# The order of the set-up groups, the split of the layer norm between VectorE and GpSimd, and the layout of inputs in a fused cross-attention and mixture-of-experts kernel

## The reference

```python
h = layernorm(x)
q = (h @ Wq).reshape(b, n, 16, 64)
k = (context @ Wk * 64 ** -0.5).reshape(b, 64, 16, 64)
v = (context @ Wv).reshape(b, 64, 16, 64)
attn = softmax(einsum('bihd,bjhd->bhij', q, k))
o = einsum('bhij,bjhd->bihd', attn, v).reshape(b, n, 1024)
x = x + tanh(g_xattn[0]) * (o @ Wo + bo)
h = layernorm(x)
probs = softmax(h.mean(axis=1) @ gate_w)          # one choice for each of the 2 sequences
top_w, top_i = top_k(probs, 2); top_w /= top_w.sum()
y = sum over the two experts e: top_w[e] * (gelu(h @ w1[e] + b1[e]) @ w2[e] + b2[e])
x = x + tanh(g_ffn[0]) * y
```

## Time and profile before

| | |
|---|---|
| median of 3 runs | 323.33 us (322.87 to 323.44) |
| the profiled execution | 322.94 us, its span 320.8 us |
| TensorE busy | 314.4 us, 98% of the span |
| VectorE busy | 233.7 us, 73% |
| ScalarE busy | 164.1 us, 51% |
| GpSimd busy | 78.8 us, 25% |
| TensorE's granted clock | full in all 40 slices |
| moved in the first three of 40 slices (8.0 us each) | 224, 395 and 197 GB/s |

### The profile page before, as it was taken

How to read it: one execution, slowest core, us unless ns; L and a number is a source line. 1 busy time by engine, 2 the same in 40 slices (tenths; PEclk the granted TensorE clock), 3 DMA queues, 4 the chain that set the end, 5 groups by cost and what they waited for, 6 DMA issues and landing times.

```text
span 320.8 us, 5745 instructions
## 1 busy us (share of the span) xinstructions
PE 314.4 (98%) x1881; PEld 272.1 (85%) x1881; DVE 233.7 (73%) x563; ACT 164.1 (51%) x577; POOL 78.8 (25%) x158
## 2 busy tenths in 40 slices
PE   7899999999999999999999999999999999999996
PEld 7887988988999999988788888888887899888896
DVE  1889997978889999999998475466667554442643
ACT  2548555686766668775466254444533442321320
POOL 1325448484455536335600000000000000000000
PEclk9999999999999999999999999999999999999999
DMA  6992000000000017600007250000020000000011
GB/s 224 395 197 4 2 3 0 0 3 3 0 0 3 0 52 246 230 1 0 2 0 263 55 208 1 0 0 0 8 102 24 2 0 2 0 0 0 2 65 65
DMA packets 20765, 17.35 MB, mean 54 GB/s; under 512 B 11068, under 2 KB 16900, under 8 KB 20612
## 3 DMA queue, kind: packets, MB, share of 16 engines
q1 hardware_dynamic: 20464, 16.51, 17.0%
q10 hardware_dynamic: 276, 0.52, 0.5%
HBM read 14.93 MB, written 2.10 MB: 53 GB/s over the span
## 4 chain that ended last, share of the span: by engine, by line
PE 88%; DVE 7%; DMA 2%; issue 1%; ACT 1%; SPq 0%; DVEq 0%
PE ps L1098 26%; PE ps L1100 26%; PE ps L1099 26%; PE ps L1183 4%; DMA xt<-in_x_dram 2%; PE ps L1272 1%; PE ps L1118 1%; DVE mx L850 1%; PE ps L1156 1%; DVE pT_lo L808 1%; PE ps L1214 1%; PE ps L1370 1%; ACT sx L580 1%; DVE stats L729 1%; DVE sm L819 1%
## 5 line engine op out<-in xcount | busy, mean ns | idle before, releaser
L667 ACT ACTIVATE gel<-ps,b1sel 128x512 f32<-128x512 f32 x64 | 43.9, 690 | 95.5 <-PE ps L1100 95.4
L1057 DVE CAST h_hi<-gel 128x512 fp32r<-128x512 f32 x64 | 28.4, 443 | 58.7 <-ACT gel L667 58.5
L580 ACT ACTIVATE sx<-ps,mx 128x64 f32<-128x64 f32 x128 | 38.3, 327 | 27.6 <-DVE mx L850 27.6
L1098 PE MATMUL ps<-yT_hi,w_hi 128*128 128x512 f32 (+1 forms) x128 | 50.5, 395 | 0.0
L1099 PE MATMUL ps<-yT_lo,w_hi 128*128 128x512 f32 (+1 forms) x128 | 50.0, 390 | 0.0
L1100 PE MATMUL ps<-yT_hi,w_lo 128*128 128x512 f32 (+1 forms) x128 | 49.9, 390 | 0.0
L1059 DVE TENSOR_TENSOR h_lo<-gel,h_hi 128x512 fp32r<-128x512 f32 x64 | 44.9, 702 | 2.2
L466 POOL TENSOR_TENSOR sx<-sx,rs 128x512 f32<-128x512 f32 x32 | 33.2, 1058 | 48.0 <-DVE rs L824 47.8
L1098 PE MATMUL ps<-h_hi,w_hi 128*128 128x512 f32 x96 | 38.4, 400 | 0.0
L1100 PE MATMUL ps<-h_hi,w_lo 128*128 128x512 f32 x96 | 37.5, 390 | 0.0
L1099 PE MATMUL ps<-h_lo,w_hi 128*128 128x512 f32 x96 | 37.4, 390 | 0.0
(11 more groups left out here) (145 smaller groups left out, 672.7 us busy)
## 6 DMA issues: line engine op xcount, KB each, us to landing
stage_w<-in_L_ffn_w_dram SPq DMA_DIRECT2D x7, 1024.0 KB, 7.3
out_dram<-xt SPq DMA_DIRECT2D x6, 256.0 KB, 2.5
wqT<-in_L_xattn_Wq_dram SPq DMA_DIRECT2D x2, 512.0 KB, 7.9
wv_sb<-in_L_xattn_Wv_dram SPq DMA_DIRECT2D x2, 512.0 KB, 9.3
wo_sb<-in_L_xattn_Wo_dram SPq DMA_DIRECT2D x1, 1024.0 KB, 13.7
xt<-in_x_dram SPq DMA_DIRECT2D x1, 1024.0 KB, 10.7
stage_w<-in_L_ffn_w_dram SPq DMA_DIRECT2D x2, 512.0 KB, 4.4
wk_sb<-in_L_xattn_Wk_dram ACTq DMA_DIRECT2D x1, 512.0 KB, 4.2
```

Of the source, the lines that this page charges most:

```text
L580: last = nc.scalar.activation(sx[:, par, c0:c0 + M], ps[:, 2 * par + 1, c0 - BANK:c0 - BANK + M], ACT.Exp, bias=mx[:, par, h:h + 1], accum ...
L667: nc.scalar.activation(gel[:, f % 4, :], ps[:, h_bank, :], ACT.Gelu, bias=b1sel[:, b, slot, f:f + 1]).then_inc(gelu_done, 1)
L1057: nc.vector.tensor_copy(h_hi[:, f % 4, :], gel[:, f % 4, :]).then_inc(hhi_ready, 1)
L1098: mm(acc, hi_w, hi_x, start=start, stop=False)
```

## The change

- Order of the set-up: TensorE, ScalarE and VectorE handle A 0 to 3 before kT 1 and A 4 to 7 behind it. The banks of the groups are dealt out anew. `tg_spread` stands ahead of the first A pair.
- Norm: x's parts are now tiles 0 and 1, 2 and 3, 4 to 7, 8 to 15. VectorE does the norm of tiles 0 and 1 in full, before the statistics of tiles 2 and 3, which move behind the `a_lo` of A 3. For tiles 2 and 3 VectorE does part 0 behind `x_low(1)` and GpSimd the refinements (`newton`) in step -1, behind `xn` of tile 1. The norms of tiles 4 to 7 and 8 to 15 stay where they were and have new numbers.
- Transfers: Wq's first half is issued ahead of Wk's second half, Wq's second half ahead of x tiles 2 and 3.
- Layout: x, Wq, Wk and Wv are laid out in memory, before the launch, so that what one transfer reads lies in one piece. The runs per partition keep their length (2 KB for Wk, Wv and x's parts of two tiles, 4 KB for Wq and four tiles).

```diff
+    def x_block(b, t0, t1):
+        first = next(n for n, (part, u0, u1) in enumerate(_X_BLOCKS) if part == b and u0 <= t0 and t1 <= u1)
+        start = sum(P * (u1 - u0) * D for _, u0, u1 in _X_BLOCKS[:first])
+        return x[start:start + P * (t1 - t0) * D].rearrange("(p t d) -> p t d", p=P, d=D)
...
-        setup_groups = [("ctxT", 0), ("kT", 0), ("kT", 1)]
-        groups = setup_groups + A0 + V0 + late_groups
+        groups = [("ctxT", 0), ("kT", 0)] + A0[:4] + [("kT", 1)] + A0[4:] + V0 + late_groups
-        GRP_BANK = dict(zip(groups, [0, 1, 2, 3, 4, 5, 6, 0, 1, 3, 4, 2, 6, 4, 5, 0, 6] + [0, 1] * len(LATE)))
+        GRP_BANK = dict(zip(groups, [0, 1, 0, 2, 3, 4, 1, 5, 6, 1, 2, 3, 6, 4, 5, 0, 6] + [0, 1] * len(LATE)))
...
-        X_PARTS = [(0, TB // 2), (TB // 2, TB), (TB, NT)]
-        X_BY_DVE = X_PARTS[1][0]
+        X_PARTS = [(0, 2), (2, TB // 2), (TB // 2, TB), (TB, NT)]
+        X_BY_DVE = X_PARTS[2][0]
...
             load_x(0, 0, 0, 2)
-            sp.dma_start(wk_sb[:, :, HD // 2:HD], Wk.rearrange("(k p) n -> p k n", p=P)[:, :, HD // 2:HD]).then_inc(ld_wk[1], 16)
+            sp.dma_start(wqT[:, 0:NP // 2, :], Wq[0]).then_inc(ld_wq[0], 16)
+            sp.dma_start(wk_sb[:, :, HD // 2:HD], Wk[1].rearrange("k p n -> p k n")).then_inc(ld_wk[1], 16)
+            sp.dma_start(wqT[:, NP // 2:NP, :], Wq[1]).then_inc(ld_wq[1], 16)
             load_x(1, 0, 2, TB // 2)
...
+                if s == -1:
+                    newton(*X_PARTS[1], rstd1, ve_x, 2)
                 if s == 1:
-                    newton(*X_PARTS[1], rstd1, ve_x, 2)
+                    newton(*X_PARTS[2], rstd1, ve_x, 3)
                     pool.sem_inc(x_rstd, 1)
...
             group("kT", 0)
+            for g in A0[:4]:
+                group(*g)
             group("kT", 1)
-            for g in A0[:7]:
+            for g in A0[4:7]:
                 group(*g)
...
             x_stats(0, range(0, 2))
-            x_stats(1, range(2, TB // 2))
             x_norm(0)
             dve.wait_ge(tg_spread, 1)
             nc.vector.tensor_copy(tg[:, :], ps[:, 7, 0:2]).then_inc(tg_ready, 1)
-            for g in A0[:6]:
+            for g in A0[:4]:
+                group(*g)
+            x_stats(1, range(2, TB // 2))
+            for g in A0[4:6]:
                 group(*g)
             x_low(0)
             for g in A0[6:]:
                 group(*g)
             x_low(1)
+            x_norm(1)
             x_stats(2, range(TB // 2, TB))
...
                     out_bias(0)
-                    x_norm(1)
+                    x_norm(2)
...
             group("kT", 0)
-            group("kT", 1)
             pe.wait_ge(rows_ready, 1)
             pe.wait_ge(tanh_done, 1)
             mm(ps[:, 7, 0:2], ones_row[:, :], tg_row[:, :], start=True, stop=True).then_inc(tg_spread, 1)
-            for i in range(0, 8, 2):
-                score_pair(i)
+            score_pair(0)
+            score_pair(2)
+            group("kT", 1)
+            score_pair(4)
+            score_pair(6)
...
+    if name == "x":
+        b, s, d = a.shape
+        a = a.reshape(b, 128, s // 128, d)
+        a = _np.concatenate([a[i, :, t0:t1, :].reshape(-1) for i, t0, t1 in _X_BLOCKS])
     if name == "L0_xattn_Wq":
-        a = a.T.reshape(-1, 128, a.shape[0]).transpose(1, 0, 2)
+        a = a.T.reshape(2, -1, 128, a.shape[0]).transpose(0, 2, 1, 3)
+    if name in ("L0_xattn_Wk", "L0_xattn_Wv"):
+        a = a.reshape(a.shape[0] // 128, 128, 2, -1).transpose(2, 0, 1, 3)
```

More of the change, by code:

```diff
@@ L17, in gated_cross_attention_moe_kernel @@
     P = 128
-    B, S, D = x.shape
-    M = ctx_tokens.shape[1]
-    HD = Wv.shape[1]
+    B, M, D = ctx_tokens.shape
+    S = out.shape[0] // B
+    HD = 2 * Wv.shape[-1]
     DH = 64
@@ L38, in gated_cross_attention_moe_kernel @@
     assert 2 * DH == P and 2 * M == P and B * M == P and TOP == 2 and NCH == 2 and KD == 2
-    x_rows = x.rearrange("b (p t) d -> p b t d", t=TB)
+    def x_block(b, t0, t1):
+        first = next(n for n, (part, u0, u1) in enumerate(_X_BLOCKS) if part == b and u0 <= t0 and t1 <= u1)
+        assert _X_BLOCKS[first] == (b, t0, t1)
+        start = sum(P * (u1 - u0) * D for _, u0, u1 in _X_BLOCKS[:first])
+        return x[start:start + P * (t1 - t0) * D].rearrange("(p t d) -> p t d", p=P, d=D)
     out_rows = out.rearrange("(b p t) d -> p b t d", b=B, t=TB)
@@ L350, in load_x @@
             def load_x(i, b, t0, t1):
-                sp.dma_start(xt[:, b * TB + t0:b * TB + t1, :], x_rows[:, b, t0:t1, :]).then_inc(ld_x[i], 16)
+                sp.dma_start(xt[:, b * TB + t0:b * TB + t1, :], x_block(b, t0, t1)).then_inc(ld_x[i], 16)
             sp.dma_start(ctx_sb[:, :], ctx_tokens.rearrange("b m d -> (b m) d")).then_inc(ld_ctx, 16)
             load_x(0, 0, 0, 2)
-            sp.dma_start(wk_sb[:, :, HD // 2:HD], Wk.rearrange("(k p) n -> p k n", p=P)[:, :, HD // 2:HD]).then_inc(ld_wk[1], 16)
+            sp.dma_start(wqT[:, 0:NP // 2, :], Wq[0]).then_inc(ld_wq[0], 16)
+            sp.dma_start(wk_sb[:, :, HD // 2:HD], Wk[1].rearrange("k p n -> p k n")).then_inc(ld_wk[1], 16)
+            sp.dma_start(wqT[:, NP // 2:NP, :], Wq[1]).then_inc(ld_wq[1], 16)
             load_x(1, 0, 2, TB // 2)
             for half in range(2):
-                blocks = slice(half * NP // 2, (half + 1) * NP // 2)
-                sp.dma_start(wqT[:, blocks, :], Wq[:, blocks, :]).then_inc(ld_wq[half], 16)
-            for half in range(2):
                 cols = slice(half * HD // 2, (half + 1) * HD // 2)
-                sp.dma_start(wv_sb[:, :, cols], Wv.rearrange("(k p) n -> p k n", p=P)[:, :, cols]).then_inc(ld_wv[half], 16)
+                sp.dma_start(wv_sb[:, :, cols], Wv[half].rearrange("k p n -> p k n")).then_inc(ld_wv[half], 16)
             load_x(2, 0, TB // 2, TB)
@@ L467, in step @@
                                                 ALU.mult).then_inc(mul_done, 1)
+                if s == -1:
+                    newton(*X_PARTS[1], rstd1, ve_x, 2)
                 if s == 1:
-                    newton(*X_PARTS[1], rstd1, ve_x, 2)
+                    newton(*X_PARTS[2], rstd1, ve_x, 3)
                     pool.sem_inc(x_rstd, 1)
                 if s == 4:
-                    newton(*X_PARTS[2], rstd1, ve_x, 3)
+                    newton(*X_PARTS[3], rstd1, ve_x, 4)
             pool.wait_ge(guess_ready, 1)
@@ L489, in _ @@
         def _(act):
-            act.dma_start(wk_sb[:, :, 0:HD // 2], Wk.rearrange("(k p) n -> p k n", p=P)[:, :, 0:HD // 2]).then_inc(ld_wk[0], 16)
+            act.dma_start(wk_sb[:, :, 0:HD // 2], Wk[0].rearrange("k p n -> p k n")).then_inc(ld_wk[0], 16)
             act.dma_start(gg[:, 0:1], g_xattn.rearrange("(o n) -> o n", o=1)).then_inc(ld_g, 16)
@@ L797, in step @@
                 if s == 4:
-                    x_norm(2)
+                    x_norm(3)
                 if s in (6, 10):
```

1 line of the change is left out of this document (added).

## The result

| | before | after |
|---|---|---|
| median, all runs beside each other | 323.07 us (322.87 to 323.44) | 324.91 us (324.02 to 325.34) |
| the profiled execution | 322.94 us, span 320.8 | 324.02 us, span 322.0 |

The changed kernel is slower: 1.0052 times the time before, interval 1.0037 to 1.0067. That is +1.84 us in the medians, where +0.94 was forecast; 324.91 lies within the range of 323.0 to 325.1 and above the forecast of 324.3. The six runs of before have their median at 323.07, not at the 323.33 of the first three, on which the 324.3 rests; so the forecast of the change is short by 0.9 and not by 0.6. The profiled execution is the fastest of the six; it lies only 1.08 us above the profiled one of before. So two things have to be read: what happens inside the profiled execution, and why most others are later.

What follows compares the result with a forecast made beforehand. VectorE was taken to set the pace up to 45.9 us, TensorE behind it. Terms -0.56 + 1.19 - 0.34 - 0.35 = -0.06, plus 1.0 for the collision, gave +0.94 us: median 324.3, range 323.0 to 325.1.

Steps and rivals of the forecast that it cites:

- The early gain: Set-up: first A pair at 8.1 and fourth at 13.60 instead of 14.16, so VectorE is free 0.56 us earlier.
- Rival 3: Set-up: Wk's second half lands after 9.94, delaying kT's second half and the A groups behind; 324.9 with collision; chance 0.12.
- Rival 2: Set-up: Wq's first half there by 7.7, first A pair at 7.8; 323.0 without collision, 323.9 with it; chance 0.10.
- The additional norm: VectorE behind `x_low(1)`: `x_norm(1)` adds 1.19 us, of which idle times of 0.34 and 0.35 take in part.
- GpSimd: GpSimd's former idle gap: `newton` from 19.5 to 23.2, then `xn` of tiles 2 and 3 from 23.3 to 25.9.
- The collision: VectorE's norm of tiles 4 to 7 falls inside GpSimd's 23.3 to 25.9 and waits: +1.0 us, bounds +0.4 and +1.4.
- Rival 1: Norm of tiles 4 to 7: VectorE's small instructions slip between GpSimd's; -0.06 to +0.4, 323.3 to 323.7 us; chance 0.26.
- My account of its stages: Norm of tiles 4 to 7: first stage +0.2, second +0.4, third and fourth +0.4 us, at least one wait in each.
- the +0.8: Norm of tiles 4 to 7: size by the Trainium skill's rule with three tensor_scalars left out, about +0.8 us.
- for which I take nothing: Input transfers: bytes and runs per partition stay, only places in memory draw together; no gain or loss counted.
- the -0.56: Sum's term for the fourth A pair at 13.60 against 14.16, counted as VectorE being free 0.56 us earlier.
- My reading of the first A pair: Set-up: Wq's first half lands at 8.0, pair starts at 8.1, not before 7.8 as kT's first half is evicted at 7.74.

Runs made afterwards that it cites:

- e2: Changed kernel with GpSimd's four instructions on tiles 2 and 3 cut to 8 of 256 columns: 323.81 us, 1.0023 of the kernel before.
- e1: Changed kernel with VectorE's norm of tiles 2 and 3 moved directly behind their statistics, into VectorE's idle gap: 323.30 us, 1.0009 of the kernel before.
- e3: Kernel before with four linked, unused 128x256 GpSimd instructions added beside VectorE's norm of tiles 4 to 7: 323.77 us, 1.0022 of the kernel before.
- e9: e4 with the norm split, tiles 0 and 1 and part 0 of tiles 2 and 3 before the first `a_lo`: 323.77 us, 1.0025 of the kernel before.
- e8: Kernel before with nine linked GpSimd memsets, which only write, beside VectorE's norm of tiles 4 to 7: 323.17 us, 1.0003 of the kernel before.
- e0: The changed kernel run once more, unchanged: 324.64 us, 1.0064 of the kernel before.
- e7: e1 without the three warm-up products (`warm_up(3)`) ahead of kT: 324.57 us, 1.0027 of the kernel before.
- e6: e1 with x, Wq, Wk and Wv in the old row layout: 323.01 us, 0.9998 of the kernel before.
- e4: Kernel before with the new layout of x, Wq, Wk and Wv alone, old order of work and transfers: 322.13 us, 0.9970 of the kernel before.
- e5: Changed kernel with x, Wq, Wk and Wv in the old row layout: 324.25 us, 1.0043 of the kernel before.
- e10: e1 with the first `warm_up(6)` lengthened to `warm_up(7)`: 323.32 us, 1.0008 of the kernel before.

## Why the prediction was right, point by point, and where a size was off

**The early gain.** The forecast of the steps in the profiled execution holds within 0.16: the first `a_lo` at 9.80 (9.96 forecast), the first A pair at 8.01 (8.1), kT's second half at 10.00 (9.94), the third pair at 12.74 (12.68), the transpose of tile 0 0.54 earlier (0.56). Rival 3, kT's second half too late by its transfer, is out: it waited for nothing. Rival 2, an A pair at 7.8, is out as well: kT's first half was evicted only at 7.92 (7.32 + 0.60).

**The additional norm.** 18.23 to 19.42 is 1.19 us, as forecast, and both idle times of VectorE that were to take it in are filled (the maximum at 20.74, forecast 20.8, without idle before it). e2 against e1 gives 0.5 for it by time.

**GpSimd.** `newton` from 19.42 to 23.06 (19.5 to 23.2), `xn` of tiles 2 and 3 from 23.14 to 25.71 (23.3 to 25.9), while VectorE's norm starts at 23.52 (23.7).

**The collision.** +1.17 was measured where 1.0 was forecast, within the bounds of 0.4 and 1.4; the sum starts at 25.88 (25.9), and TensorE passes the place of the earlier trace rows at 46.82 instead of 45.87, +0.95 for +0.94. Rival 1, VectorE slips through, would have left the norm under 1.8 us. e2 takes the collision out alone and e3 puts it in alone, so for this point the cause is shown and not only argued; 0.8 and 0.7 are its prices in the medians. My account of its stages was rough: I had one wait in the first, and none of its three instructions was much longer; the second stage had two.

The Trainium skill (SBUF — State Buffer, Who interferes with whom) names two ways into the contention: two SBUF inputs against a GpSimd read, and tensor_scalar when it runs in a two-port mode. I had left the second out of the +0.8 that I gave by it. In the traces instructions of both kinds wait: L718, L720 and L723, all tensor_scalars, in after; L714, L716 and L718, all with two inputs, in e9. Whether the tensor_scalars ran in such a mode no trace here shows. With these three counted in, all eight instructions of the norm are exposed, as my 1.0 from the rows had it. The memsets of e8 agree with its rule that a GpSimd instruction that only writes doesn't hold up an instruction with two SBUF inputs; the one tensor_scalar beside them took 0.25 instead of 0.17.

**Where a size was off: the start of kT, and the layout "for which I take nothing".** In the medians the change costs 1.84 and not 0.95. The term of the sum that fails is the -0.56, which took the first 5 us as fixed. They aren't: at the transpose of tile 0 the same order and layout gave -0.54 in after, but -0.01 in e1 and e2 and +0.32 in e0. In the five traces with the old layout the context lands 2.3 to 2.9 us after its issue, in the eight with the new one 3.1 to 3.7, and kT's first half starts at 4.95 to 5.47 in the former and at 5.23 to 6.15 in the latter. Wk's first half lands 4.2 to 4.3 us after its issue in the former and 4.5 to 5.0 in the latter. And in some executions of either layout TensorE's matmuls before 6 us are slow. Each of the three sets kT's start in some trace: Wk's first half in e1 and e7, the context and slow warm-ups in e0, slow warm-ups alone in e2 and e6. In the old order a late start costs nothing, since kT's second half waited for Wk anyway and the chain goes over x tiles 2 and 3 (e4). In the new order the first A pair stands 2.78 us behind kT's start (after, e0 and e1), and there is no wait left that could hide it. My reading of the first A pair asked when Wq lands, and took the other condition, kT's eviction at 7.74, from one execution, as a bound on how early it could be; the question to ask was how late it can be. It was the binding one: at 8.01 TensorE waits for nothing that a transfer releases, and 7.92 is when the eviction ends.

A second term is missing from the sum, for the end of the kernel. From VectorE's last instruction to the end of the span it is 2.35 to 2.39 us in the four traces in which VectorE does the norm of tiles 0 to 3 in full (before, e3, e4, e8) and 2.55 to 2.77 in the nine with that norm split. e9 has the old order, and e5 and e6 the old layout, so these 0.2 us come with the split of the norm; by what way, no run shows.

That 324.91 lies within the range is in part luck. It is the 324.9 that I gave rival 3 with a collision: the early gain gone. It is gone in e0's trace, which is close to the median, but by the start of kT and not, as rival 3 has it, by the landing of Wk's second half.

**What the layout is worth was missed altogether.** I found no term for it and no row against it. e4 shows -1.0 us for the old order, more than the collision, and of the other sign. In the changed kernel it is lost. My reading of why: what comes sooner (x tiles 2 and 3, Wk's second half) is what that order no longer waits for, and what comes later, the context and Wk's first half, is what it hangs on.

**The account by parts,** in medians, each against the kernel before beside it: the layout -1.0 (e4); the new order, with GpSimd's newly gained norm in the gap, on top of it +1.2 (e1 at +0.24, e4 at -0.99); the place of the additional norm +0.5 (e2 against e1); the collision +0.8 (e0 against e2). Unrounded the sum is +1.6, that of e0, as it must be, since each part is the difference of two neighbours in the row before, e4, e1, e2, e0; it is no check. The first runs of the changed kernel gave 1.8. Of the 1.2 of the order the traces of e1 and e4 have 0.88 from tile 0 to VectorE's last instruction, and 0.4 behind it, in the end of the kernel; 0.2 of that recurs in every trace with the norm split, so that much belongs to the split and not to the order. For the part before tile 0 the two timelines of TensorE say: from the start of kT to the transpose of tile 0 it is 14.72 - 5.23 = 9.49 us in after and 14.37 - 5.89 = 8.48 in e4. Of the 1.0 between them, the gaps of 0.42 and 0.69 behind the two evictions of kT stand on one side and the one of 0.37 behind `a_lo` on the other, 0.74 net. The other 0.27 is 0.34 more for kT's two halves and the gates' product (4.41 us in two pieces in after, 4.07 in one in e4), less 0.07 in the A pairs. Each half of kT now has its eviction on TensorE's path, where one after the other hid it.

**What stays open.** Why the context and Wk's first half land later under the new layout, and which of the four inputs does it: each tensor's layout was not tried by itself. Why TensorE's matmuls before 8 us take their double time in some executions and not in others, with either layout (1.48 to 1.49 us for `warm_up(3)` in e0, e2, e4 and e6, 0.83 in after, e1 and e8, 1.07 to 1.34 in before, e3, e5, e9 and e10): the granted clock of the stretches up to 8 us is 1.00 in all of them that I looked at. Why the end of the kernel takes 0.2 us longer with the split norm. Why most runs of the changed kernel are later than its first trace is shown by one more trace (e0) and argued for the rest. Nor was it tried whether an order that leaves kT's halves together, and only moves the transfers, would gain on e4.

## What to carry to other kernels

- Before work is moved to another engine's idle time, lay the two timelines on each other at its new place: here four GpSimd instructions of 0.61 us doubled a chain of eight small VectorE ones, and the same happened once more in e9 when a norm came earlier. If VectorE is the pace, such a chain belongs where GpSimd is silent or writes only.
- A wait that an order removes was also a cushion: ask of the first product of the new order what it hangs on, and how far that varies between executions. One traced execution, above all the fastest, can't tell: kT started at 5.23 in it, and at up to 6.15 in others.
- A change of several parts may hide a good one. The layout by itself was the only part worth keeping, 322.13 us.

## What the runs showed of the hardware that was not expected

- Inputs laid out so that one transfer reads one piece came at 392 to 406 GB/s in the stretch from 3 to 8 us (eight traces), against 288 to 330 (five traces), with the same bytes and the same runs of 2 and 4 KB. The first small transfer landed after 3.1 to 3.7 us instead of 2.3 to 2.9, Wk's first half after 4.5 to 5.0 instead of 4.2 to 4.3.
- VectorE's small instructions wait beside GpSimd's reads up to the end of the GpSimd instruction that runs: 0.15 to 0.17 us becomes 0.47 to 0.58. It was not the same ones each time: tensor_scalars in after, TENSOR_TENSORs in e9, a tensor_scalar and a scalar_tensor_tensor in e3.
- TensorE's first matmuls can take nearly twice their time (3.75 for 2.05, e7) in a stretch whose granted clock is given as 1.00. In the first 8 us of this kernel the durations tell it, and the clock doesn't.
